# The second layer norm moved behind the third masked heads on VectorE, and its sum with the residual written to a buffer of its own

## The reference, cut to what matters

```
x  = L0_attn_x                                    # (16, 512, 128)
xn = layernorm(x)
x  = x + ssm(xn) + top1_experts(xn)               # layer 0
xn = layernorm(x)
x  = x + attn(xn) + recurrent(xn)                 # layer 1
...
attn(xn):       o = Y @ Wout.T + xn               # Y: 16 heads with decay and level weights
                return (o - mean(o)) * rsqrt(var(o) + 1e-5) * ln_g + ln_b
recurrent(xn):  c = sigmoid(..) * c + sigmoid(..) * tanh(..)      # over 16 sequences, one step each
                return tanh(xn @ wo.T + c_final @ uo.T + bo)
```

## Time and profile before

| | |
|---|---|
| median of 3 runs | 1060.34 us (1059.51 to 1061.62) |
| the profiled execution | 1059.19 us, its span 1057.4 us |
| mean granted TensorE clock | 0.991 |
| PE busy | 1010.9 us (96%) |
| DVE busy | 891.1 us (84%) |
| ACT busy | 705.8 us (67%) |
| POOL busy | 162.0 us (15%) |
| transfers | 27.62 MB, 8.0% of the 16 engines' span on SP's queue |

### The profile page before, as it was taken

How to read it: one execution, slowest core, us unless ns; L and a number is a source line. 1 busy time by engine, 2 the same in 40 slices (tenths; PEclk the granted TensorE clock), 3 DMA queues, 4 the chain that set the end, 5 groups by cost and what they waited for, 6 DMA issues and landing times. The chain is left out here.

```text
span 1057.4 us, 20086 instructions
## 1 busy us (share of the span) xinstructions
PE 1010.9 (96%) x6700; PEld 676.2 (64%) x6700; DVE 891.1 (84%) x2122; ACT 705.8 (67%) x1525; POOL 162.0 (15%) x171
## 2 busy tenths in 40 slices
PE   7899999999999999999999999999999999999984
PEld 4666757666675766757576675766667576675753
DVE  6797897979889797997979889797988979799686
ACT  4693957849486593957749395683948659395692
POOL 0020110111101011110201111011110101111076
PEclk9999999999999999999999999999999999999997
DMA  4000000000000000000000000000000000000526
GB/s 153 20 3 11 2 20 11 0 30 0 20 10 20 10 0 30 0 20 10 0 30 0 30 0 20 10 0 30 0 20 10 17 12 0 30 0 20 179 76 193
DMA packets 31908, 27.62 MB, mean 26 GB/s; under 512 B 1552, under 2 KB 25744, under 8 KB 31760
## 3 DMA queue, kind: packets, MB, share of 16 engines
q1 hardware_dynamic: 31888, 27.37, 8.0%
HBM read 15.57 MB, written 11.80 MB: 26 GB/s over the span
## 5 line engine op out<-in xcount | busy, mean ns | idle before, releaser
L1013 ACT ACTIVATE gx<-p 128x512 f32<-128x512 f32 x256 | 145.9, 596 | 11.5 <-PE p L552 6.9
L1829 POOL TENSOR_TENSOR vp<-vdw,e 128x256 f32<-128x256 f32 (+3 forms) x80 | 60.7, 789 | 556.7 <-ACT e L1062 556.7
L550 PE MATMUL p<-x1Th,Gl 128*128 128x512 f32 x256 | 119.9, 468 | 0.3 <-ACT gx L1013 0.3
L961 ACT ACTIVATE gelu<-p,bias_u 128x512 f32<-128x512 f32 x32 | 22.0, 688 | 124.5 <-PE p L493 124.5
L552 PE MATMUL p<-x1Th,Gh 128*128 128x512 f32 x256 | 100.8, 394 | 0.0
L551 PE MATMUL p<-x1Tl,Gh 128*128 128x512 f32 x256 | 100.2, 391 | 0.0
L672 PEld LDWEIGHTS p<-vbd,pair 128*128 128x128 f32 x512 | 62.0, 191 | 40.4 <-issue 26.8
L612 PEld LDWEIGHTS p<-rs,GT 128*128 128x128 f32 x512 | 60.8, 192 | 21.4 <-ACT ms L1094 13.4
L672 PE MATMUL p<-vbd,pair 128*128 128x128 f32 x512 | 73.3, 286 | 0.0
L626 PE MATMUL p<-gx,x1T 128*32 128x512 f32 x512 | 68.2, 604 | 2.0 <-ACT gx L1013 0.8
L967 ACT ACTIVATE sm<-mv 128x4 f32<-128x4 f32 x32 | 6.6, 205 | 92.0 <-DVE mv L1338 91.7
(11 more groups left out here) (277 smaller groups left out, 2609.9 us busy)
## 6 DMA issues: line engine op xcount, KB each, us to landing
xin<-in_x SPq DMA_DIRECT2D x16, 256.0 KB, 2.8
hx_scratch<-vdw SPq DMA_DIRECT2D x15, 256.0 KB, 2.6
res_scratch<-res SPq DMA_DIRECT2D x14, 256.0 KB, 2.1
gx<-in_weights SPq DMA_DIRECT2D x1, 1216.0 KB, 9.4
vp<-hx_scratch SPq DMA_DIRECT2D x4, 256.0 KB, 3.6
GT<-res_scratch SPq DMA_DIRECT2D x4, 256.0 KB, 3.7
out<-vp SPq DMA_DIRECT2D x4, 256.0 KB, 3.4
W<-in_weights SPq DMA_DIRECT2D x1, 746.0 KB, 10.6
```

What stands on the lines that cost most here:

```text
L550: pe.matmul(head_bank(h)[:, :], tile(Gl, h), x1Th[:, :], start=True, stop=False)
L1013: act.activation(tile(gx, h, T), head_bank(h)[:, :], ACT.Copy).then_inc(R["gx_copied"], 1)
L1829: last = pool.tensor_tensor(view(vp[:, at:at + 128 * count], "p (s h e) -> p s h e", s=count, e=HD), spread(v.unsqueeze(1), [128, count, H ...
```

## The change

`norm2(i - 1)` moves on DVE from behind `pair_weights(i, 1)` to behind `level_sum(i, 2)`. A new buffer `normed` takes the sum that `finish` makes, and the store to DRAM reads it, so `residual` waits no longer for the store but for `res_ready`, which the same engine raised one instruction earlier. `finish` waits in turn until the store of the stage before has freed `normed`. SP issues the store of `vdw` ahead of the store of the sum. POOL sets `normed` to zero once at the start, which also raises `normed_free` for the first time.

```diff
--- before.py
+++ after.py
@@ -189,6 +189,7 @@
         hx_dram = nc.dram_tensor("hx_scratch", (B, 128, T), fp32, kind="Internal").ap()
         res_dram = nc.dram_tensor("res_scratch", (B, 128, T), fp32, kind="Internal").ap()
         res = sb("res", T)
+        normed = sb("normed", T)
         WQ, WK = w("Wq"), w("Wk")
 
 
@@ -200,7 +201,7 @@
             + [w("Win"), W[:, wat["Wout0"][0]:wat["b2"][0]], tile(spare, 0, T), tile(spare, 1, T)]
         end_hx = free[0:9] + [tile(vp, n, T) for n in range(4)] \
             + [cell[:, :], W[:, wat["gates_c"][0]:wat["gates_c"][0] + T], free[18]]
-        end_res = free[9:18] + [tile(GT, n, T) for n in range(4)] + [lam[:, 0:T], res[:, :], x1[:, :]]
+        end_res = free[9:18] + [tile(GT, n, T) for n in range(4)] + [lam[:, 0:T], normed[:, :], x1[:, :]]
         c_out = sp0
 
 
@@ -219,7 +220,7 @@
             gx_ps gx_copied cgrow_ready diff_ready diff_abs decay_ready own_steps lamx_ready nodes_ready nodesT_ready
             s_ps lam_ps dlam_ready w_ready vbd_zero vbd_ready y1_ps ym_ready y2_ps lev_ps lev_ready levsum_ready
             yt_ready ytT_ps ytT_ready wo_ps ob_ready st2_ready mv2_ready ln2_ready r2_ready n_ready
-            res_init skip_ready ng_ready res_ready res_stored f_ps i_ps g_ps tf_ready ti_ready tg_ready ig_ready c_ready
+            res_init skip_ready ng_ready res_ready normed_free f_ps i_ps g_ps tf_ready ti_ready tg_ready ig_ready c_ready
             cp_ps cp_ready end_loaded0 end_loaded1 end_loaded2 end_sum end_tanh end_add end_pool_add end_stored""".split()
         R = {n: sem(n) for n in names}
 
@@ -279,7 +280,7 @@
 
             def store_res(i):
                 sp.wait_ge(R["res_ready"], i + 1)
-                sp.dma_start(row(res_dram, i), res[:, :]).then_inc(R["res_stored"], 16)
+                sp.dma_start(row(res_dram, i), normed[:, :]).then_inc(R["normed_free"], 16)
 
             def load(group, hx, rs):
 
@@ -291,9 +292,9 @@
             def stages(i, j):
                 if j is not None:
                     load_x(j)
+                store_hx(i)
                 if later(i):
                     store_res(i - 1)
-                store_hx(i)
 
             def store(b, end_view, src):
                 sp.dma_start(view(out[b], "(k p) d -> p k d", p=128)[:, end_view], view(src, "p (k d) -> p k d", d=D)[:, end_view])\
@@ -301,7 +302,7 @@
 
             def last():
 
-                sp.wait_ge(R["res_stored"], 16 * (B - 2))
+                sp.wait_ge(R["normed_free"], 16 * (B - 1))
                 sp.wait_ge(R["hx_stored"], 16 * (B - 1))
                 sp.wait_ge(R["x1_ready"], B)
                 sp.wait_ge(R["u1_ps"], B)
@@ -1706,8 +1707,6 @@
                 if i is not None:
                     own_heads(i, 0)
                     pair_weights(i, 1)
-                    if later(i):
-                        norm2(i - 1)
                     level_sum(i, 0)
                     tile_sum(i, 0)
                 if j is not None:
@@ -1722,6 +1721,8 @@
                 if i is not None:
                     own_heads(i, 2)
                     level_sum(i, 2)
+                    if later(i):
+                        norm2(i - 1)
                     pair_weights(i, 3)
                     tile_sum(i, 2)
                     level_sum(i, 3)
@@ -1812,7 +1813,7 @@
 
                 pool.wait_ge(R["x1_ready"], j + 1)
                 if later(j):
-                    pool.wait_ge(R["res_stored"], 16 * j)
+                    pool.wait_ge(R["res_ready"], j)
                 pool.tensor_tensor(view(res[:, :], "p (k d) -> p k d", d=D), view(x1[:, :], "p (k d) -> p k d", d=D),
                                    spread(w("lnbias").unsqueeze(1), [128, TILES, D]), ALU.add).then_inc(R["res_init"], 1)
 
@@ -1846,7 +1847,8 @@
                 pool.tensor_tensor(view(skip[:, :], "p (k d) -> p k d", d=D), view(skip[:, :], "p (k d) -> p k d", d=D),
                                    spread(w("lng").unsqueeze(1), [128, TILES, D]), ALU.mult).then_inc(R["ng_ready"], 1)
                 pool.wait_ge(R["ng_ready"], i + 1)
-                pool.tensor_tensor(res[:, :], res[:, :], skip[:, :], ALU.add).then_inc(R["res_ready"], 1)
+                pool.wait_ge(R["normed_free"], 16 * i + 16)
+                pool.tensor_tensor(normed[:, :], res[:, :], skip[:, :], ALU.add).then_inc(R["res_ready"], 1)
 
             def last_residual():
 
@@ -1887,8 +1889,11 @@
                 residual(i)
                 keep_skip(i)
 
-            schedule(pool, lambda: pool.memset(vbd[:, :], 0.0).then_inc(R["vbd_zero"], 1),
-                     stages, last)
+            def first():
+                pool.memset(vbd[:, :], 0.0).then_inc(R["vbd_zero"], 1)
+                pool.memset(normed[:, :], 0.0).then_inc(R["normed_free"], 16)
+
+            schedule(pool, first, stages, last)
 
 
 # ---- launch: one core; inputs and outputs as the reference has them ----
```

## The result

| | before | after |
|---|---|---|
| median | 1059.92 us (4 runs) | 1041.78 us (4 runs) |
| all runs | 1058.83 to 1061.62 | 1041.22 to 1043.34 |
| ratio to before | | 0.9831, interval 0.982 to 0.9843 |

The change makes the kernel 18.1 us faster, 1.30 us in each of the 14 loop turns. The prediction was 1044.2 us, a gain of 16.1 against the median of 1060.34 it had. The time lies inside the stated range of 1041.5 to 1051.5, but only 0.3 us above its lower end.

A forecast was written before the change was run, and what follows sets the result against it. TensorE, busy 96% of the span, was taken to bound the kernel, waiting for VectorE. Per turn 0.71 + 0.26 + 0.18 = 1.15 us; 14 turns give 16.1, and 1060.34 - 16.1 = 1044.2 us, range 1041.5 to 1051.5.

The forecast's parts named there:

- The mechanism: Mid-stage in the loop: VectorE's norm, 1.02 us, delays the second masked heads; moving it removes TensorE's 0.71 us wait.
- what a turn wins: 1.15 us: First chunk sums to sum0 in each loop turn: 0.71 + 0.26 + 0.18 us less on TensorE.
- the upper bound: First chunk sums to sum0: loop stage 16.95 us against first stage 15.64, 1.31 us a turn, 18.3 us in all.
- the forecast's cases: Loop turns shorter by 1.0 to 1.31 us, giving 1042.0 to 1046.3 us; 63 in 100.
- The contention: First gate's L1438 on VectorE, slowed beside GpSimd's add L1849: 1.57 us against 0.74, so 0.83 us won by VectorE.
- 2 us too late: Chain from norm through finish and refill to sum0: how late it would end if the refill still waited for the store.
- The slack of 0.3 us: Before sum0: GpSimd's refill lets it start at about 414.7, TensorE at 415.01, so the moved chain fits with 0.3 us.
- its sum to 414.65: GpSimd's chain after the moved norm: start 410.65, sum 412.01 to 413.28, refill 413.36 to 414.65 in the stage's time.
- The partial relief: Rival: only the second chunk sums' bracket goes, 1050.4 us, or L1438 stays slow, 1051.2 us; 17 in 100.
- The late chain: Rival: GpSimd's chain before sum0 ends later than worked out; 0.5 us too late gives 1047.0 us; 8 in 100.
- That nothing is won: Rival: time won before out0 is given back behind it by a wait, 1060.3 us; 7 in 100.
- The slower rival: Rival: VectorE holds up GpSimd's three operations between norm and sum0, 2.9 us late, 1080.7 us; 5 in 100.

The follow-up runs named there:

- The norm inside the third level_sum: On top of the change, first heads masked before the level weights, and the norm between the third level_sum's product and reduction: 1037.59 us, ratio 0.9801.
- the held-back GpSimd: The changed kernel with the norm put back in its old place, and GpSimd starting finish only after the second gate's product: 1047.92 us, ratio 0.9891.

## Why the prediction was right, and where it was off

Two more rows of PE's timeline before the change are needed here, the groups ahead of the second and of the third chunk sums, in the stage of the earlier trace rows:

```profile
404.49 0.39 PE L493 MATMUL p<-mask_b,expert_b 128*128 128x128 bf16 x4
...
409.95 0.39 PE L493 MATMUL p<-mask_b,expert_b 128*128 128x128 bf16 x4
```

- **The mechanism held.** VectorE was late in the middle of the stage, and TensorE's path got the lateness back. The wait ahead of the second chunk sums is gone, L1439 is 745 ns everywhere, the refill follows the sum at once, and sum0 names TensorE.
- **The mis-sized term is what a turn wins: 1.15 us, measured 1.30.** I expected 0.71, 0.26 and 0.18 us in the three stretches from the first chunk sums to the second, to the third and to sum0. They got shorter by 0.78 (6.37 to 5.59), 0.36 (4.75 to 4.39) and 0.17 (5.83 to 5.66), 1.31 together. So the total came out near the upper bound, 18.1 against 18.3 us, and below the 1042.0 us that the forecast's cases began with. I had 1.31 in hand as the difference to the first stage, and put 0.16 of it aside as the price of register waits in the loop. The changed kernel's stage takes the first stage's 15.64 us exactly, so nothing of it was register work. Most of it was waiting without a bracket. A bracket counts only the time in which the engine is empty by the profile; when nobody is late, the next group starts before the last one's modelled end (401.75 + 0.39 = 402.14, against the start at 402.07). Before the change the second chunk sums started 0.77 us later than they could (404.49 to 405.58, 1.09 us behind the start of L493, against 401.75 to 402.07, 0.32 us, now), with a bracket of 0.71, and the third 0.06 us (409.95 to 410.33, 0.38 us), with none. The norm inside the third level_sum shows the same: 0.28 us came back where the bracket said 0.21.
- **The contention was rightly counted, and it was worth more than I gave it.** I wrote that TensorE can't use those 0.83 us. With the norm moved that is nearly so, as an estimate from the changed kernel's rows: 0.83 us later, the third masked heads would end at 406.41, just ahead of the chunk sums at 406.46, and the product of the third level_sum at 406.94, just behind the start of the levels at 406.82. No run has the norm moved and the contention kept. But the held-back GpSimd shows that without the contention, with the norm in its old place and the buffer there, 11.4 of the 18.1 us are won: the two reliefs are 1.85 us together, for a wait of the second chunk sums that needed less than one. The move alone shows the other half, L1438 at 744 to 749 ns in all 32 runs, with the old buffer.
- **The two parts need each other**, as the prediction said: the move alone is 1.0274 of before, the buffer alone 1.0144, both together 0.9831. The prediction had "2 us too late" for the chain without the buffer, and 2.07 was measured; the cost in time, 29 us against before, was more than this gives, since the clock's share was not in it.
- **The slack of 0.3 us was under 0.1**: the refill ends 0.14 us ahead of sum0, the hop to VectorE included, and a norm 0.60 us later made sum0 0.57 us later. Half of the error is that TensorE came 0.16 us earlier than I had it. The hop with the new register instruction took 0.18 us (the bracket of L1851), 0.1 more than the plain hop of 0.08. The prediction says that it takes 0.08 for the register instruction, but its sum to 414.65 leaves it out: 1.36 us is the plain pitch. The hop from the refill's end to sum0 was 0.10 to 0.11 us in the runs where sum0 waited for it, and I had allowed 0.05.
- **The rivals.** The partial relief (1050.4 or 1051.2) did not happen: L1438 was slow only because of its neighbour. The late chain did not happen, but it was less than 0.1 us away, as the norm one group later shows; that the forecast held against it was in part luck. That nothing is won fell with the 18.1 us, which went through out0 to the end of the turn. The slower rival, GpSimd held up in its new place, fell as its counter-evidence said: the operations took 1.26 to 1.28 us beside PSUM reads and reductions. No experiment made VectorE hold it up there.

## What to carry to other kernels

When an engine that others wait for is late, ask for each of its slow instructions who ran beside it: the same 0.8 us can be had by moving work of a third engine that nobody waits for. Measure a wait as the difference of starts against a turn in which nobody was late, since brackets show less. And when a chain loses its cover, work out its end to the tenth of a microsecond before moving it, and move it with what shortens it.

## What the runs showed of the hardware

- A two-input SBUF instruction of VectorE of 128x512 took 0.69 to 0.75 us alone, and 1.57 to 1.68 us when it met a GpSimd add, ending 0.55 to 0.56 us behind the add. GpSimd's own add behind it went from 1.27 to 1.52 us, its copy from 0.61 to 1.07 (the buffer alone).
- An idle of 2.0 us of TensorE was followed by a mean granted clock of 0.51 to 0.65 over the next 3.5 us in eleven turns of the move alone, 1.5 us of loss each, and by full clock in three turns with the same idle. An idle of 1.69 us (the buffer alone) was followed by a fall of the clock in one turn of 13, which took 1.3 us longer. I had not expected so short an idle to cost more than itself. Waits of about half a microsecond (the norm one group later) were followed by no such loss.
